# Linear attention and a routed expert layer on one core: the drain between them reordered, the expert bias moved to VectorE, one VectorE step later in each group

## The reference

```python
q, k, v = split(x @ w_qkv)                       # 128 -> 3 x 128, then 16 heads of 8
qf = elu1(q @ proj); kf = elu1(k @ proj)         # elu1(a) = a + 1 if a > 0 else exp(a)
kv = sum_n kf[n] (x) v[n];  ks = sum_n kf[n]     # per head: 32 x 8 and 32
attn = (qf @ kv) / (qf @ ks + 1e-8)
x = layernorm(x + attn @ w_out + b_out)
e = argmax(x @ wr + br)                          # one of 8 experts for each token
y = gelu(x @ w1[e] + b1[e]) @ w2[e] + b2[e]      # 128 -> 512 -> 128
out = layernorm(x + y)
```

## Time and profile before

| | |
|---|---|
| median of 3 runs | 234.96 us (234.77 to 235.1) |
| the profiled execution | 234.93 us, its span 233.2 us |
| TensorE matmul busy | 202.8 us, 87% |
| VectorE busy | 154.7 us, 66% |
| ScalarE busy | 140.2 us, 60% |
| GpSimd busy | 133.4 us, 57% |
| mean granted TensorE clock | 0.962 |

### The profile page before, as it was taken

How to read it: one execution, slowest core, us unless ns; L and a number is a source line. 1 busy time by engine, 2 the same in 40 slices (tenths; PEclk the granted TensorE clock), 3 DMA queues, 4 the chain that set the end, 5 groups by cost and what they waited for, 6 DMA issues and landing times.

```text
span 233.2 us, 5949 instructions
## 1 busy us (share of the span) xinstructions
PE 202.8 (87%) x1727; PEld 159.0 (68%) x1734; DVE 154.7 (66%) x530; ACT 140.2 (60%) x366; POOL 133.4 (57%) x171
## 2 busy tenths in 40 slices
PE   7989999999799998898888389899899999999700
PEld 2668888888555554545442279798799999999600
DVE  1577686877476999889989233247557677777720
ACT  3488887878477576866564045455466667666400
POOL 8329284646500104776768617655776588888770
PEclk9999999999999999999999679999999999999955
DMA  4899999999760000111011467650477678874100
GB/s 119 217 379 409 414 408 410 411 414 375 220 178 0 0 6 12 35 35 47 27 35 46 147 175 217 195 138 20 154 221 220 201 229 236 233 182 133 35 6 0
DMA packets 28416, 40.45 MB, mean 173 GB/s; under 512 B 3497, under 2 KB 18126, under 8 KB 28384
## 3 DMA queue, kind: packets, MB, share of 16 engines
q1 hardware_dynamic: 26112, 35.80, 47.5%
q0 software_dynamic: 2272, 4.27, 5.3%
HBM read 17.95 MB, written 22.56 MB: 174 GB/s over the span
## 4 chain that ended last, share of the span: by engine, by line
PE 55%; issue 13%; POOL 12%; DVE 8%; DMA 4%; ACT 4%; SPq 1%; POOLq 1%; DVEq 0%; ACTq 0%
PE pair L753 15%; PE pair L299 12%; PE pair L768 10%; POOL sorted_rows L504 9%; PE bank L615 4%; PE bank L768 4%; PE pair L746 2%; DMA x_all<-sorted_rows 1%; DVE qexp L969 1%; PE pair L585 1%; POOL rstd L476 1%; ACT qexp L829 1%; DMA w_slot<-in_L_ffn_w_dram 1%; PE bank L595 1%; PE pair L765 1%
## 5 line engine op out<-in xcount | busy, mean ns | idle before, releaser
L912 ACT ACTIVATE qfeat<-pair,w_sb 128x128 f32<-128x128 f32 x156 | 44.7, 368 | 29.1 <-PE pair L753 28.5
L753 PE MATMUL pair<-xsT,w_slot 128*128 128x128 f32 x312 | 42.4, 280 | 1.7 <-DMA w_slot<-in_L_ffn_w_dram 1.2
L504 POOL DMA_INDIRECT sorted_rows<-x,dest x32 | 33.4, 1043 | 17.1 <-DVE dest L1115 9.9
L753 PEld LDWEIGHTS pair<-xsT,w_slot 128*128 128x128 f32 x312 | 38.7, 195 | 2.4 <-issue 2.4
L299 PE MATMUL pair<-wkv_part,xT_all 128*128 128x256 f32 x192 | 33.8, 320 | 2.0 <-ACT vals L839 0.8
L299 PEld LDWEIGHTS pair<-wkv_part,xT_all 128*128 128x128 f32 x192 | 28.3, 188 | 5.5 <-issue 5.5
L768 PE MATMUL pair<-w_sb,qfeat 128*128 x232 | 31.5, 279 | 0.0
L534 POOL TENSOR_TENSOR ksum<-kfeat 128x512 f32<-128x512 f32 x12 | 16.5, 1372 | 24.9 <-DVE kfeat L978 24.9
L525 POOL DMA_INDIRECT out_dram<-x_all x26 | 26.3, 1010 | 7.0 <-issue 5.7
L768 PEld LDWEIGHTS pair<-w_sb,qfeat 128*128 128x128 f32 x232 | 28.2, 192 | 0.9
L476 POOL TENSOR_TENSOR rstd<-var_eps,minus_half 128x4 f32<-128x4 f32 x8 | 8.3, 1041 | 31.4 <-DVE var_eps L1051 31.4
(11 more groups left out here) (181 smaller groups left out, 405.8 us busy)
## 6 DMA issues: line engine op xcount, KB each, us to landing
sorted_rows<-pad_rows SPq DMA_DIRECT2D x11, 1584.0 KB, 22.9
w_slot<-in_L_ffn_w_dram SPq DMA_DIRECT2D x39, 256.0 KB, 3.1
x_all<-in_L_attn_x_dram SPq DMA_DIRECT2D x8, 256.0 KB, 5.4
w_sb<-in_L_ffn_w_dram SPq DMA_DIRECT2D x4, 512.0 KB, 14.0
x_all<-sorted_rows SPq DMA_DIRECT2D x26, 66.0 KB, 2.6
xs<-sorted_rows SPq DMA_DIRECT2D x13, 66.0 KB, 2.3
w_sb<-in_L_ffn_b_dram SPq DMA_DIRECT2D x1, 512.0 KB, 7.2
sorted_rows<-x,dest POOLq DMA_INDIRECT x32, 2.5
```

The source lines that it names most:

```text
L504: g_.indirect_dma_start(out=sorted_rows, out_offset=bass.IndirectOffsetOnAxis(ap=dest[:, ring, i:i + 1], axis=0), in_=x1[:, ring, i, :], i ...
L753: last = mm(h_bank[t % 2][:, k * P:(k + 1) * P], w1_slot[:, t % WB, k * P:(k + 1) * P], xsT[:, t % 2, :], start=True, stop=True)
L912: a_.activation(hT[:, t % 2, k * P:(k + 1) * P], h_bank[t % 2][:, k * P:(k + 1) * P], ACT.Gelu, bias=w2_sb[:, bass.ds(w_at[t] + (FF + D + ...
```

## The change

On VectorE, `shift_of` and `rows` move behind `normalise` in every group step, the score steps move one long operation later each, and `add_x` and the first `statistics` move ahead of `choose`. In the drain the first table is made in another order, with e_tab ready after step 8 (TAB_E), and SP loads w1 of tiles 0 to 3 at that point, ahead of its wait for the scatters. From then on it issues the weights two tiles ahead of the rows; the weights of tiles 13 and 14 wait for the second table, and stand ahead of the wait for the last scatters. On TensorE project(7), four of the busy-keeping matmuls and ranks(6) stand ahead of turn(0); ranks(7) comes two tiles earlier. GpSimd no longer does layer norm: ScalarE does it for group 6 ahead of tile 0's copy and for group 7 one tile at a time behind tile steps 0 to 3. The bias matmul is gone, and VectorE adds the bias of all tiles. VectorE's second table is spread over tiles 2 to 5, and the first four batches are normalised one tile later.

```diff
-        TAB_A, TAB_B = 14, 16
+        TAB_E, TAB_A, TAB_B = 8, 14, 16
-        def offset(eng, kind, table, t, most):
+        def offset(eng, kind, table, t, most, first=TAB_A):
             if t == 0:
-                eng.wait_ge(tab_step, TAB_A)
+                eng.wait_ge(tab_step, first)
...
-        NORMALISED_IN = {7: 0, 10: 1, 13: 2, 16: 3, 20: 4, 23: 5, ...}
-        BIASED_BY_DVE = range(10, NT)
+        NORMALISED_IN = {8: 0, 11: 1, 14: 2, 17: 3, 20: 4, 23: 5, ...}
...
+            def load_weights(t):                       # SP
                 reach(sp, hid_pre, t - WB + 1)
-                at = offset(sp, ENG.SP, e_tab, t, (E - 1) * FF)
+                at = offset(sp, ENG.SP, e_tab, t, (E - 1) * FF, TAB_E)
                 sp.dma_start(w1_slot[:, t % WB, :], ...).then_inc(w1_loaded[t % WB], 16)
+            for t in range(4):
+                load_weights(t)
             for i in range(XR):
                 sp.wait_ge(scattered[i], 16 * GT * len(range(i, GA, XR)))
             for t in range(NA):
                 load_rows(t)
-
+                if 4 <= t + 2 < NA:
+                    load_weights(t + 2)
+            for t in (NA, NA + 1):
+                load_weights(t)
             for i in range(XR):
                 sp.wait_ge(scattered[i], 16 * GT * G // XR)
             sp.wait_ge(res_ready, G)
             for t in range(NA, NT):
                 load_rows(t)
+                if t + 2 < NT:
+                    load_weights(t + 2)
...
             inverse_deviation(G - 2)                   # GpSimd
-            layer_norm(G - 2)
             scatter(G - 3, range(0, 2))
             token_numbers(G - 1)
             inverse_deviation(G - 1)
             scatter(G - 3, range(2, GT))
-            layer_norm(G - 1)
...
                 reach(pe, yx_ready, t - 3)             # down(t)
-                if t not in BIASED_BY_DVE:
-                    mm(y_bank[t % 4][:, 0:D], ones_row[:, :], w2_sb[0:1, bass.ds(w_at[t] + FF, D)], start=True, stop=False)
...
             stay_awake(12, bank[2])                    # TensorE, drain
+            project(G - 1)
+            stay_awake(4, bank[2])
+            ranks(G - 2)
             turn(0)
             weights_of(0)
             up(0)
-            project(G - 1)
             turn(1)
             weights_of(1)
             tile_step(0)
-            ranks(G - 2)
             tile_step(1)
+            ranks(G - 1)
             tile_step(2)
             tile_step(3)
-            ranks(G - 1)
...
                     exp_q(s, 1)                        # ScalarE, group step
+                    exp_q(s, 2)
                 if 0 <= s - 3 < G:
                     layer_norm(s - 3)
-                if s < G:
-                    exp_q(s, 2)
...
             a_.preload_act_table_set("gelu_and_others")
+            layer_norm(G - 2)
             keep_rows(0)
             gelu(0)
             keep_rows(1)
-            for s in range(NT):
+            for s in range(GT):
+                tile_step(s)
+                norm_tile(G - 1, s)
+            for s in range(GT, NT):
                 tile_step(s)
...
                     newton_first(s - 2)                # VectorE, group step
-                if route:
-                    shift_of(s - 3)
                 if row:
                     row_numbers(s - 4)
                 if attn:
                     newton_second(s - 2)
-                if route:
-                    scale_scores(s - 3)
                 if row:
                     next_rows(s - 4)
                     pick_rows(s - 4)
                 if attn:
                     normalise(s - 2)
+                if route:
+                    shift_of(s - 3)
+                if row:
+                    rows(s - 4)
                 if s:
                     q_features(s - 1, 3)
...
```

More of the change, by code:

```diff
@@ L476, in inverse_deviation @@
                 g_.tensor_tensor(rstd[:, par, :], var_eps[:, par, :], minus_half[:, :], ALU.pow).then_inc(rstd_ready, 1)
-            def layer_norm(g):
-                par, ring = g % 2, g % XR
-                pool.wait_ge(shift_ready, g + 1)
-                pool.wait_ge(rstd_ready, g + 1)
-                for i in range(GT):
-                    last = g_.tensor_scalar(x1[:, ring, i, 0:D], res[:, par, i, :], rstd[:, par, i:i + 1], shift[:, par, i:i + 1],
-                                            ALU.mult, ALU.add)
-                last.then_inc(x1_ready, 1)
             def token_numbers(g):
@@ L768, in down @@
                     last = mm(y_bank[t % 4][:, 0:D], hT[:, t % 2, k * P:(k + 1) * P],
[L769 removed]
+                              w2_sb[:, bass.ds(w_at[t] + k * D, D)], start=(k == 0), stop=(k == FC - 1))
                 last.then_inc(y_pre, 1)
@@ L878, in layer_norm @@
                 act.wait_ge(number_ready, g + 1)
+                last = a_.activation(x1[:, g % XR, i, 0:D], res[:, par, i, :], ACT.Identity,
+                                     bias=shift[:, par, i:i + 1], scale=rstd[:, par, i:i + 1])
+                if i == GT - 1:
+                    last.then_inc(x1_ready, 1)
+            def layer_norm(g):
                 for i in range(GT):
-                    last = a_.activation(x1[:, g % XR, i, 0:D], res[:, par, i, :], ACT.Identity,
-                                         bias=shift[:, par, i:i + 1], scale=rstd[:, par, i:i + 1])
-                last.then_inc(x1_ready, 1)
+                    norm_tile(g, i)
             def group_step(s):
@@ L1155, in group_step @@
                 if attn:
-                    for i in range(GT):
+                    for i in range(1, GT):
                         statistics(s - 2, i)
@@ L1304, in _ @@
+            statistics(6, 3)
             offsets_of(first)
             assert done[0] == TAB_A
+            for i in range(GT):
+                moments(6, i)
             add_epsilon(6)
@@ L1315, in _ @@
             shift_of(6)
+            weights_of(0)
             scale_scores(6)
+            add_x(7)
             bias_scores(6)
+            add_x_score(7)
             best_score(6)
+            statistics(7, 0)
             is_best(6)
+            statistics(7, 1)
             count_best(6)
+            statistics(7, 2)
             choose(6)
-            add_x(7)
-            add_x_score(7)
-            for i in range(GT):
-                statistics(7, i)
+            statistics(7, 3)
             for i in range(GT):
@@ L1328, in _ @@
             add_epsilon(7)
-            add_row(0)
+            weights_of(1)
             row_numbers(6)
-            row_statistics(0)
             next_rows(6)
             pick_rows(6)
+            rows(6)
+            add_row(0)
+            shift_of(7)
+            add_bias(0)
+            scale_scores(7)
+            row_statistics(0)
+            bias_scores(7)
             row_moments(0)
-            rows(6)
+            best_score(7)
+            weights_of(2)
+            is_best(7)
@@ L1337, in _ @@
             add_row(1)
-            shift_of(7)
+            count_best(7)
+            add_bias(1)
+            choose(7)
             row_statistics(1)
-            scale_scores(7)
             row_moments(1)
-            bias_scores(7)
+            weights_of(3)
             add_row(2)
-            best_score(7)
-            row_statistics(2)
-            is_best(7)
-            row_moments(2)
-            count_best(7)
-            add_row(3)
-            choose(7)
-            row_statistics(3)
@@ L1392, in _ @@
-            add_row(8)
+            add_row(5)
             first_weights_of(rest)
-            row_statistics(8)
+            add_bias(5)
             offsets_of(rest)
-            row_moments(8)
             assert done[0] == TAB_A + TAB_B
-            for s in range(9, NT + 1):
+            row_statistics(5)
+            row_moments(5)
+            weights_of(7)
+            for s in range(6, NT + 1):
                 tile_step(s)
```

106 lines of the change are left out of this document (46 added, 60 removed).

## The result

| | before | changed |
|---|---|---|
| median (range, runs) | 234.87 us (234.72 to 235.1, 4) | 224.89 us (224.32 to 225.48, 4) |
| ratio | | 0.9575 (0.9542 to 0.9607) |
| profiled execution, its span | 234.93, 233.2 us | 225.48, 223.8 us |
| mean granted TensorE clock | 0.962 | 0.961 |

What follows compares the result with a forecast made beforehand. TensorE bounds the tiles, VectorE the group loop. Gains of 5.7 us by up(1) reach 13.9 by up(38), less 0.3 for stores: 234.93 - 13.6 = 221.3 us, own range 220 to 222.7, 8 in 10 219.8 to 225.5.

Steps and rivals of the forecast that it cites:

- The group loop: Group loop: six VectorE waits for rstd ahead of shift go, 3.0 us saved, attnT of group 7 at 124.4.
- The order at the first turn: Drain: projection at 125.1, turn(0) at 128.6 behind the rank, up(0) at 129.3; 5.7 us gained by up(1).
- The step that failed: Tiles: up(38) at 131.9 + 37 x 1.89 + 1.3 = 203.2, 13.9 us earlier than before.
- the rival: Drain: the clock falls, nearly 7 us at half speed cost 3.3, giving 224.6; chance 0.2.
- The hole for the rank of group 7: Early tiles: ranks of group 7 still stop TensorE, 1.2 us before, 1.3 now.
- The bias: Tiles 0 to 9: bias off TensorE, 2.50 to 1.89 us each, 6.1 us saved; the addition fits on VectorE.
- tile 13's rows: Tile 13: rows issued at 148.3, landed 151.5, wanted at 154.0; the stall goes with 2.5 us to spare.
- GpSimd's stores: Stores to the end: some 60 us of work, fits by 0.7 us; 0.3 taken for short waits (0 to 2).
- Layer norm on ScalarE: Drain and early tiles: eight activations of 0.41 us for groups 6 and 7, no table load added, no cost.

Runs made afterwards that it cites:

- e5_loop_only: The kernel before with only the new order of the group loop (VectorE's group step, ScalarE's third exponential ahead of layer norm): 233.25 us, ratio 0.99.
- e9_project_back: The changed kernel with project(7) and its 4 idle-filling matmuls back behind up(0), ranks(6) behind tile step 0: 225.78 us.
- e4_rank_later: The changed kernel with ranks(7) one tile step later on TensorE, behind tile step 2: 223.48 us.
- e6_bias_only: The kernel before with the bias of all tiles added by VectorE and no bias matmul, nothing else: 233.42 us, ratio 0.9925.
- e11: The e8_route_early kernel with the first four batches normalised one tile step earlier, as before the change: 221.31 us.
- e2_fill_gelu: The changed kernel with 7 idle-filling matmuls behind turn(1), where TensorE waits for gelu(0) and tile 1's copy: 223.18 us.
- e8_route_early: The changed kernel with group 7 routed in VectorE's idle time ahead of add_row(0), ranks(7) and 6 idle-filling matmuls behind turn(1): 220.86 us.
- e1: The changed kernel with 8 instead of 4 idle-filling matmuls between project(7) and ranks(6): 225.39 us.
- e3: The changed kernel with 17 instead of 12 idle-filling matmuls ahead of project(7), 8 instead of 4 ahead of ranks(6), 7 behind turn(1): 223.47 us.
- e12: The e8_route_early kernel without the 6 idle-filling matmuls behind turn(1): 222.29 us, ratio 0.945.

## Why the prediction was right and wrong

- *The group loop* was right: 3.2 us at attnT (forecast 3.0), and e5_loop_only shows it at the end of the kernel, 3.7 in the profiled run.
- *The order at the first turn* was right within 0.3 us at each step. But its worth was not: I credited 5.7 us at the start of up(1), of which 3.2 are the loop's and the other 2.5 are the drain's new order, the projection's place above all. up(1) did move by 5.2 us, only to run at half clock; e9_project_back, without the move, has up(1) 2.6 us later and ends within 0.1 us.
- *The step that failed* is the sentence that up(1) to up(38) takes 37 tiles at 1.89 and one hole, all at full clock. I had argued that with the hole of 3.77 us gone the fall goes too. The fall stayed, with holes of 1.56 us at most: the rival, given 0.2, priced 3.3 and measured 3.0 in the profiled pair, 1.7 between the medians. That the median came within 0.3 us of the rival's 224.6 is in part luck: by the medians the fall costs half of the rival's price, and other errors of the sum fill the rest (0.4 at up(1), 0.7 at the rank, 0.7 behind it, less 0.6 in the tail). The rival deserved the larger chance: I had read myself that TensorE would work some 4 of 8 us there (3.9 from 124 to 132, as measured), sparser than any other stretch but the one where the clock had fallen, and I let one long gap stand for the cause because it was the one thing the row named.
- *The hole for the rank of group 7* was mis-sized: 1.3 us in the sum, 1.95 in the distance between ups. The hole was read as its idle time alone, without the rank and the turn that then stand by themselves.
- *The bias*: the 6.1 us came, less 0.6 hidden by the rank's wait and 0.6 found again behind (4.9 in the profiled pair, 6.2 between medians). That the tiles' time reached the end rests on tile 13's rows, where I was right that the stall goes, but not with 2.5 us to spare: layer norm of group 7 ended 4 us late and the rows were issued 6 us late (154.54 for 148.3). It held since TensorE was late too; in e4_rank_later, where it was 2 us sooner, the rows of tile 15 did stop it for 0.39 us. I named the scatters and GpSimd as what must be in time, and the rows of before were held last by the second table (4.1 us of SP's wait). The change makes that table by 149.4 (I said 145), 12.4 us earlier than e6_bias_only; there the wait for it and the clock's fall behind it took 2.9 us.
- *GpSimd's stores* were right: 60 us of work, nearly without waits, and not the bound (e11).
- *Layer norm on ScalarE* at no cost: nothing in the traces speaks against it, no table load and no wait of TensorE, but no run tests it alone. Its late end for group 7 leaves GpSimd idle for 9 us, yet tile 13's rows still come in time.
- The parts in spans of single profiled runs: loop 3.7, bias with the early table 4.9, the remaining 0.8 of 9.4 us is all else in the drain. With the medians' 6.2 for the bias nothing is left of it, so the 0.8 is not shown.

Open: why single tiles behind up(3) take 0.1 to 0.2 us more, two in the changed kernel and in e2_fill_gelu, one in e8_route_early, each at another place; why the profiled runs of e1, e3, e11 and e12 reach the projection 0.5 to 0.7 us later with the same loop; and why the first low stretch of the clock is 10.2 us long in e6_bias_only.

## What to carry to other kernels

Add up TensorE's busy time over a few microseconds around each hole, and don't ask only how long the longest hole is: a change that turns one long gap into three short ones may leave the clock as low as it was. When a part is taken off the bound engine, find what the next stall waits for by its last releaser (here a small table on VectorE, not the transfers), since the same edit gave 1.6 us with that stall and 4.9 without, in the profiled runs. And look where an engine that others wait for is itself idle: moving group 7's routing there gave 2.3 us, more than the projection's new place (0 to 0.9).

## What the runs showed of the hardware

- The start of the fall differed by kernel, from 126.9 to 132.5 us, and so did the low stretch: nearly 7 us in the kernels before and after and in most variants, about 3.4 in e12_route_early_nofill (worked out from its two windows), although the changed kernel and this one both had holes of 1.1 to 1.6 us ahead of it, and 10.2 in e6_bias_only, where the clock fell a second time behind a stall of 2.07 us.
- Matmuls that nobody reads cost nothing where TensorE waited: seven of them, 1.69 us, fit into the gelu's wait, and turn(2) behind them stayed at 131.85.
- Where the hole was longest (5.33 us, e9_project_back), the slow stretch was over by up(1), and the kernel ended no later in the profiled run than with holes of 1.6 us at most.
- The bias matmul of 128 columns with one row (two records, 0.48 us) cost 0.61 us a tile, two thirds of the eight matmuls of an up or a down (0.89).
